# First stage of a four-batch DeltaNet attention and RWKV feed-forward block: a second pair of projection banks, the gates' bias moved to ScalarE, the first norms moved to VectorE, and a new order of steps

## What is computed

```
h  = layernorm(x)
q, k, v = silu(causal_conv4(h @ W{q,k,v}.T))              # 4 taps per channel
beta    = sigmoid(h @ Wb.T)
delta   = delta_rule(l2norm(q), l2norm(k), v, beta)       # a scan over time
local_s, local_m, local_l = causal FIRs of v, 3, 15 and 63 taps per channel
probs = softmax((h @ gate_w + gate_b) / exp(log_temp))    # 5 per head and row
probs = probs * (1 - 5 eps) + eps,  eps = clip(eps_param, 0, 0.2)
o = p0*local_s + p1*local_m + p2*local_l + p3*delta + p4*v
x = x + layernorm(rmsnorm(o) * norm_w @ Wo.T)
r = sigmoid((mu_r*y + (1-mu_r)*y_prev) @ W_r), kk = relu((mu_k*y + (1-mu_k)*y_prev) @ W_k)^2,  y = layernorm(x)
x = x + layernorm(r * (kk @ W_v))
```

## Time and profile before

| | |
|---|---|
| median of 3 runs | 615.87 us (606.55 to 617.87) |
| profiled execution, its own time | 611.72 us |
| its span, first to last instruction | 609.9 us |
| mean granted TensorE clock, share of 2.4 GHz | 0.943 |
| busy: TensorE, VectorE, GpSimd, ScalarE | 84%, 76%, 55%, 45% of the span |

### The profile page before, as it was taken

The page is one execution under the profiler, slowest core; times in us unless marked ns, Lnnn a source line. Parts: engine busy times, 40 slices in busy tenths (PEclk is TensorE's granted clock), DMA queues, the critical chain, the costliest instruction groups (busy, mean ns, idle before and its releaser), DMA issues.

```text
span 609.9 us, 23551 instructions
## 1 busy us (share of the span) xinstructions
PE 512.3 (84%) x9580; PEld 407.8 (67%) x9580; DVE 465.3 (76%) x1182; ACT 276.6 (45%) x688; POOL 336.4 (55%) x408
## 2 busy tenths in 40 slices
PE   2888848999889789798999979899787899888764
PEld 1666636666667567677777767777666777777553
DVE  3788684655589673788899989899768879889863
ACT  5788882111355443435455444454342444433421
POOL 9966202877702440486626378464278776566622
PEclk9999997999999795899999999999888899999978
DMA  9729444699344425341444624165343244333101
GB/s 286 204 71 258 144 139 121 156 225 227 64 73 75 81 63 100 52 72 37 98 88 92 121 52 80 44 120 105 67 72 69 51 104 76 70 80 80 37 17 35
DMA packets 155707, 61.10 MB, mean 100 GB/s; under 512 B 125009, under 2 KB 147409, under 8 KB 155601
## 3 DMA queue, kind: packets, MB, share of 16 engines
q1 hardware_dynamic: 155600, 59.61, 44.5%
HBM read 40.62 MB, written 18.95 MB: 98 GB/s over the span
## 4 chain that ended last, share of the span: by engine, by line
PE 29%; DVE 23%; issue 17%; POOL 13%; SPq 7%; DMA 6%; ACT 3%; POOLq 0%; DVEq 0%; ACTq 0%
PE bank L1864 6%; PE bank L1639 5%; DVE cva L1126 4%; DVE arena L1236 3%; PE bank L1553 3%; POOL arena L659 3%; PE bank L1901 3%; DVE arena L1350 3%; PE bank L1718 2%; DVE arena L1365 2%; DVE arena L1338 2%; POOL seq L650 2%; POOL seq L561 2%; PE bank L1758 2%; POOL seq L648 2%
## 5 line engine op out<-in xcount | busy, mean ns | idle before, releaser
L659 POOL TENSOR_TENSOR arena<-arena,neg_half 128x2 f32<-128x2 f32 (+1 forms) x64 | 61.2, 956 | 148.4 <-DVE arena L1325 88.1
L1236 DVE SCALAR_TENSOR_TENSOR arena<-bank,small,arena 128x256 f32<-128x256 f32 x192 | 89.9, 481 | 15.5 <-ACT arena L898 10.6
L1210 DVE TENSOR_TENSOR seq<-bank,seq 128x384 f32<-128x384 f32 x64 | 35.2, 556 | 30.3 <-PE bank L1639 19.4
L606 POOL TENSOR_TENSOR arena<-seq,powers 128x16 f32<-128x16 f32 x16 | 48.6, 3040 | 17.0 <-DVE seq L1252 17.0
L1639 PE MATMUL bank<-arena 128*64 128x192 f32 x512 | 50.4, 340 | 3.9 <-DVE seq L1210 1.6
L1126 DVE SCALAR_TENSOR_TENSOR cva<-bank,small,cva 128x256 f32<-128x256 f32 x96 | 40.3, 477 | 15.1 <-ACT cva L775 14.8
L577 POOL TENSOR_TENSOR seq<-seq 128x256 f32<-128x256 f32 x32 | 23.3, 729 | 48.2 <-DVE seq L1210 48.2
L1639 PEld LDWEIGHTS bank<-arena 128*64 128x64 f32 x512 | 35.4, 140 | 13.4 <-issue 6.3
L1350 DVE TENSOR_SCALAR arena<-arena 128x256 f32<-128x256 f32 x64 | 31.7, 536 | 16.0 <-POOL arena L659 16.0
L898 ACT ACTIVATE arena<-bank,small 128x256 f32<-128x256 f32 x64 | 29.7, 467 | 26.2 <-PE bank L1718 26.2
L1718 PE MATMUL bank<-arena,w_k 128*128 128x268 f32 x128 | 34.5, 412 | 4.4 <-issue 3.1
(11 more groups left out here) (170 smaller groups left out, 1364.5 us busy)
## 6 DMA issues: line engine op xcount, KB each, us to landing
arena<-v_scratch SPq DMA_DIRECT2D x64, 128.0 KB, 3.3
arena<-fl SPq DMA_DIRECT2D x32, 192.0 KB, 6.4
arena<-fms SPq DMA_DIRECT2D x32, 192.0 KB, 6.8
arena<-xnT_scratch SPq DMA_DIRECT2D x32, 134.0 KB, 3.1
arena<-x SPq DMA_DIRECT2D x32, 128.0 KB, 2.9
gram_scratch<-arena SPq DMA_DIRECT2D x32, 128.0 KB, 2.4
out<-arena SPq DMA_DIRECT2D x32, 128.0 KB
xnT_scratch<-seq SPq DMA_DIRECT2D x2, 1027.0 KB, 6.7
```

The costliest lines, as they stand in the source:

```text
L606: pool.tensor_tensor(rk, ssel[:, slot_of(n)], powers[:, :, :], ALU.pow).then_inc(s["norms"], 1)
L659: pool.tensor_tensor(dst, src, half8 if k == U else neg_half[:, 0:k], ALU.pow).then_inc(s[dst_sem], 1)
L1210: nc.vector.tensor_tensor(fprod[:, q % (2 * FPAIRS), :], bank[fir_bank(q)][:, 0:2 * ROW], fgate[:, q // (TILES // 2), :], ALU.mult).then_i ...
L1236: nc.vector.scalar_tensor_tensor(cv[:, t], ps[:, :, j:j + C], conv_w[:, 1 - t // 2, t % 2, j:j + 1], cv[:, t], ALU.mult, ALU.add).then_inc ...
```

## The change

Only the first stage and the gates are touched, and one stretch between them and the filters.

- The projections use two pairs of banks in turn, (2, 3) for even q and (7, 1) for odd q, and two rows buffers, `cva` and the new `cvx`. `a_proj` now waits for the convolution two blocks back, and `a_tap` for the SiLU of four instructions back. In return the transposes of x have only bank 0.
- `a_norm` of batch 0, blocks 0 and 1, is done by VectorE (`a_first`), right behind `a_row_stats(0, 0)`. GpSimd does the others.
- The gates' bias and temperature are applied in `a_gT_out` on ScalarE, by per-partition scale and bias with the function Identity. The ten VectorE instructions of L1174 fall away; one that multiplies the bias stands in the new `gates_prepared`, behind the first convolution, with the two of L1170 and L1171.
- `gates_mixed`, the last six steps of the softmax, stands inside the sequence (in the same place of VectorE's order).
- The order of the steps on TensorE, ScalarE and VectorE is another one. ScalarE's order per batch differs most at `a_win_out` 4 and 5 and `a_vb` 4 and 5, which now stand before the Exp and the last two SiLUs.
- Ahead of the filters, ScalarE copies `fgate` before it waits for the stores to DRAM, and VectorE does not wait for the stores.

```diff
+        def a_bank(q, oh):
+            return bank[(2, 3, 7, 1)[2 * (q % 2) + oh]]
+        def a_row(q, oh):
+            return (cvx if q % 2 else cva)[:, oh, :]
...
             def rows_of(b, h):
-                if b >= 2:
-                    sp.wait_ge(s["a_normed"], 8 * (b - 2) + 4 * h + 4)
+                if b == 2 and h == 0:
+                    sp.wait_ge(s["a_first"], 4)
+                elif b >= 2:
+                    sp.wait_ge(s["a_normed"], 8 * (b - 2) + 4 * h)
...
             def a_norm(b, q):
+                if b == 0 and q < 2:
+                    return
...
             def a_tap(b, i):
                 act.wait_ge(s["a_proj"], b * 8 + i + 1)
-                act.wait_ge(s["a_vT"], b * 8 + (i - 1 if i >= 2 else 0))
+                if 8 * b + i >= 4:
+                    act.wait_ge(s["a_vT"], b * 8 + i - 3)
...
                 act.wait_ge(s["a_gturn"], b)
-                act.activation(gT, bank[6][:, 0:2 * P], ACT.Copy).then_inc(s["a_gT"], 1)
+                act.wait_ge(s["g_step"], G_READY)
+                act.activation(gT, bank[6][:, 0:2 * P], ACT.Identity, bias=gate_bias, scale=inv_temp).then_inc(s["a_gT"], 1)
...
             # ScalarE, the new order of one turn
             def sequence(b):
                 if 0 <= b - 1 < B:
+                    a_xT_out(b - 1, 1)
+                if 0 <= b - 2 < B:
+                    a_vb(b - 2, 5)
+                    a_vb(b - 2, 4)
+                    gates_exp(b - 2)
+                    a_silu(b - 2, 6)
+                    a_silu(b - 2, 7)
+                if 0 <= b - 1 < B:
+                    a_tap(b - 1, 0)
+                    a_tap(b - 1, 1)
+                    a_xT_out(b - 1, 2)
+                    a_silu(b - 1, 0)
+                    a_xT_out(b - 1, 3)
+                    a_silu(b - 1, 1)
+                    a_tap(b - 1, 2)
+                    a_tap(b - 1, 3)
+                if 0 <= b - 2 < B:
+                    a_vb(b - 2, 6)
+                    a_win_out(b - 2, 6)
+                    a_vb(b - 2, 7)
+                    a_win_out(b - 2, 7)
+                if 0 <= b - 1 < B:
+                    a_silu(b - 1, 2)
+                    a_silu(b - 1, 3)
+                    a_tap(b - 1, 4)
+                    a_gT_out(b - 1)
+                    a_tap(b - 1, 5)
+                    a_win_out(b - 1, 0)
+                    a_vb(b - 1, 0)
+                    a_win_out(b - 1, 1)
+                    a_vb(b - 1, 1)
+                    a_win_out(b - 1, 2)
+                    a_silu(b - 1, 4)
+                    a_tap(b - 1, 6)
+                    a_silu(b - 1, 5)
+                    a_tap(b - 1, 7)
+                    a_vb(b - 1, 2)
+                    a_vb(b - 1, 3)
+                    a_win_out(b - 1, 3)
                 if 0 <= b < B:
+                    a_xT_out(b, 0)
                 if 0 <= b - 1 < B:
                     a_win_out(b - 1, 4)
                     a_win_out(b - 1, 5)
...
             act.wait_ge(s["a_win"], 8 * B)
+            for pr in range(PAIRS):
+                act.wait_ge(s["fgate_mm"], pr + 1)
+                act.activation(fgate[:, pr, :], bank[6 + pr][:, 0:2 * ROW], ACT.Copy).then_inc(s["fgate"], 1)
             act.wait_ge(s["a_gturn"], B)
             for par in ("even", "odd"):
                 act.wait_ge(s[f"xT_{par}_stored"], 16 * 2)
                 act.wait_ge(s[f"vb_{par}_stored"], 64 * 2)
-            for pr in range(PAIRS):
-                act.wait_ge(s["fgate_mm"], pr + 1)
-                act.activation(fgate[:, pr, :], bank[6 + pr][:, 0:2 * ROW], ACT.Copy).then_inc(s["fgate"], 1)
...
+            def a_first(b):
+                if b == 0:
+                    dve.wait_ge(s["a_rs"], 1)
+                    for m in range(4):
+                        nc.vector.tensor_scalar(xna[:, m, :], xa2[0][:, m, :], mv_a[:, m, 0:1], rs_a[:, m:m + 1],
+                                                ALU.subtract, ALU.mult).then_inc(s["a_first"], 1)
...
             # VectorE, the new order: row_stats(0,0), a_first(0), row_stats(0,1), row_stats(1,0), then for each batch
+                    a_conv(b - 26, 0)
+                    gates_ready(b - 26)
+                    a_row_stats(b - 25, 1)
+                    a_conv(b - 26, 1)
+                    a_conv(b - 26, 2)
+                    a_gates(b - 26)
+                    gates_shift(b - 26)
+                    a_conv(b - 26, 3)
+                    gates_sum(b - 26)
+                    a_row_stats(b - 24, 0)
...
-                for g in range(5):
-                    for pr in range(PAIRS):
-                        last = nc.vector.tensor_scalar(gates[:, g, pr, :], gates[:, g, pr, :], gb[:, pr, g:g + 1],
-                                                       inv_temp[:, pr:pr + 1], ALU.add, ALU.mult)
-                then(last)
+                then(nc.vector.tensor_tensor(gate_bias, gate_bias, inv_temp, ALU.mult))
...
             dve.wait_ge(s["a_gate"], B)
-            for par in ("even", "odd"):
-                dve.wait_ge(s[f"xT_{par}_stored"], 16 * 2)
-                dve.wait_ge(s[f"vb_{par}_stored"], 64 * 2)
...
             def a_xT(b, q):
+                if 4 * b + q >= 1:
+                    pe.wait_ge(s["a_xT_out"], b * 4 + q)
...
             def a_proj(b, q):
-                    if b or q:
-                        pe.wait_ge(s["a_conv"], b * 24 + 6 * (q - 1) + 5 + oh)
+                    if 4 * b + q >= 2:
+                        pe.wait_ge(s["a_conv"], b * 24 + 6 * (q - 2) + 5 + oh)
...
             # TensorE, the new order of one batch (its block 0's transposes stand one turn earlier)
+                    a_xT(b - 11, 1)
+                    a_proj(b - 11, 0)
+                    a_xT(b - 11, 2)
+                    a_xT(b - 11, 3)
+                    a_proj(b - 11, 1)
+                if 0 <= b - 12 < B:
+                    a_win(b - 12, 6)
+                    a_win(b - 12, 7)
+                if 0 <= b - 11 < B:
+                    a_gate(b - 11)
+                    a_proj(b - 11, 2)
+                    a_win(b - 11, 0)
+                    a_win(b - 11, 1)
+                    a_gate_turn(b - 11)
+                    a_win(b - 11, 2)
+                    a_proj(b - 11, 3)
+                    a_win(b - 11, 3)
+                    a_win(b - 11, 4)
+                if 0 <= b - 10 < B:
+                    a_xT(b - 10, 0)
+                if 0 <= b - 11 < B:
+                    a_win(b - 11, 5)
```

More of the change, by code:

```diff
@@ L110, in build @@
         norm_w = small[:, 28:29]
-        gb = small[:, 29:39].rearrange("p (r g) -> p r g", r=PAIRS)
-        inv_temp = small[:, 39:41]
-        mix_eps = small[:, 41:43]
+        gate_bias = small[:, 29:30]
+        inv_temp = small[:, 30:31]
+        mix_eps = small[:, 31:33]
         neg_half = sb("neg_half", [P, U])
@@ L562, in a_norm, with sequence @@
                                        ALU.subtract, ALU.mult).then_inc(s["a_normed"], 1)
[L564 to L568, removed]
+            def sequence(b):
+                if 0 <= b - 57 < B:
+                    a_power(b - 57, 0)
+                    a_norm(b - 57, 0)
+                    a_norm(b - 57, 1)
+                    a_power(b - 57, 1)
+                    a_norm(b - 57, 2)
+                    a_norm(b - 57, 3)
+            for b in range(0, 61):
+                sequence(b)
             def fir_sum(h):
@@ L1103, in a_row_stats @@
                 dve.wait_ge(rows_in_sem(b, h), 16 * (b // 2) + 16)
-                if b:
-                    dve.wait_ge(s["a_normed"], 8 * (b - 1) + 4 * h + 4)
+                if b == 1 and h == 0:
+                    dve.wait_ge(s["a_first"], 4)
+                elif b:
+                    dve.wait_ge(s["a_normed"], 8 * (b - 1) + 4 * h)
                 for m in tiles:
@@ L1138, in a_gates, with gates_ready @@
                             nc.vector.tensor_copy(dst[HH[1 - hh], b, :, pr, :, :, par], src[:, NG * h:NG * h + NG]).then_inc(s["a_gate_out"], 1)
+            def gates_ready(b):
+                if b == 0:
+                    gates_prepared()
             def gates_shift(b):
@@ L1166, in _, with gates_prepared @@
             mx4 = gmax[:, :, :].rearrange("p r (w o) -> p o r w", o=1).broadcast_to((P, 5, PAIRS, BLK))
-            def gates_shifted():
-                dve.wait_ge(s["a_gate_out"], 8 * B)
+            def gates_prepared():
+                dve.wait_ge(s["small_in"], 16)
                 dve.wait_ge(s["g_exp"], 1)
@@ L1536, in a_xT @@
             def a_xT(b, q):
-                pe.wait_ge(s["a_normed"], b * 8 + 2 * q + 2)
-                if 4 * b + q >= 2:
-                    pe.wait_ge(s["a_xT_out"], b * 4 + q - 1)
+                if b == 0 and q < 2:
+                    pe.wait_ge(s["a_first"], 2 * q + 2)
+                else:
+                    pe.wait_ge(s["a_normed"], b * 8 + 2 * q - 2)
+                if 4 * b + q >= 1:
+                    pe.wait_ge(s["a_xT_out"], b * 4 + q)
                 for hf in range(HALVES):
```

(7 more changed lines are left out.)

115 lines of the change are left out of this document (41 added, 74 removed).

## The result

The changed kernel takes 608.38 us, median of 20 runs (605.98 to 614.51, and one of 943.74 that nothing on record explains), against 614.92 for the kernel before in as many (606.55 to 620.95). By these medians it is 6.5 us faster. The ratio of the two is 0.9935, 95% interval 0.9910 to 0.9959: 4.0 us faster, within 2.5 to 5.5. This ratio counts of each kernel only the fast runs, those within 1.5% of its fastest, 19 of the changed kernel's and 12 of the other's, which leaves out the upper part of the runs of before and so makes the difference smaller. Forecast were 5.6 us and 608; the two measures stand on either side of the 5.6. The profiled execution has a span of 606.5 us against 609.9.

A forecast was written before the change was run, and what follows sets the result against it. The projection, tap and convolution loop was taken as the limit, three engines close behind. Gains of 1.5 at the start, 2.5 by the last batch, 4.4 at the transposes, 5.6 with 1.18 for stores: 606.1 or 610.3, predicted 608, range 598 to 616.

The forecast's parts named there:

- What bounds it, and the batch: First stage: the new banks open the loop, ScalarE's order (tap 4 behind SiLU 3) closes another; 17.5 us a batch against 17.62.
- E: End of convolution 1 of a batch in the first stage; forecast at 23.0, 40.5 and 58.0 us.
- The start: Batch 0: four norms on VectorE bring the first projection 2.1 us earlier; 1.5 us gained at the end of convolution 1.
- tile 4: Fifth filter tile, from which TensorE is almost full; forecast to start at 97.1 against 102.73, 5.6 us earlier.
- The moved bias: Gates: two pointer operands add 0.17 us to each `a_gT_out`; removing ten VectorE instructions leaves ScalarE late next.
- rival 4: At `a_gT_out`: Identity needs another table than SiLU, so loads cost 10.3 us, 4.7 over the gain, 616.4; chance 0.05.
- Hidden loads: First stage: x for batch 3's first half, behind `v_store(0)`, lands at 48.3, 1.7 us ahead of its statistics.
- The tail: Behind the convolutions: Exp no longer waits for VectorE; last SiLU ends at 87.2 against 91.0, transposes start 4.4 us earlier.
- Had it stayed up: TensorE's clock stays up ahead of the filters: fifth filter tile at 93.9, 8.8 us gained, 603; chance 0.18.
- The stores: Ahead of the filters: removing VectorE's and ScalarE's waits for stores, 6.42 us idle, is worth 1.2 us.
- To the end: Behind the fifth filter tile: later work follows by dependence, so its 5.6 us gain carries to the end unchanged.
- a stretch behind 165 us that is longer or shorter by over a microsecond: Late part of the trace, from 165 us on: such a change in its length would show the forecast wrong.

The follow-up runs named there:

- Exp last: The changed kernel with the gates' Tanh and Exp behind the last two SiLUs on ScalarE: 608.55 us, ratio 0.9841 to the kernel before.
- TensorE kept busy: The changed kernel with 11 matmuls of unused result where TensorE idles ahead of the last transposes: 606.80 us, ratio 0.9802 to the kernel before.
- the delay: The changed kernel with ten useless copies of 1024 columns on ScalarE ahead of its first fgate copy: 620.83 us, ratio 1.0057 to the kernel before.

## Why the prediction was right, and where it was not

**What bounds it, and the batch.** Right in time: E 17.38 and 17.36 us apart, forecast 17.5; without statistics 16.84, forecast 16.9. The reason was half of it. "ScalarE's order does" hold tap 4 back, but with that opened it waited for TensorE's third projection, behind the gates' product. Only both moved gave 16.64 (the projection ahead alone was not run). I had looked for what is late next on ScalarE and not on TensorE.

**The start.** The gain at E of batch 0 is 1.84 us (22.66 against 24.50), forecast 1.5: a norm on VectorE took 0.35 us, not 0.41. But taking the norms back cost 2.6 us there: E was at 25.26, 0.76 behind the kernel before, about what the three steps of `gates_prepared` take ahead of convolution 1 in that run (20.04 to 20.89). So the norms bring 2.6 us and the new order takes part of it back. The rest of the 3.8 at tile 4 is the slow clock of that execution. What the norms would bring in the old order was not run.

**The moved bias.** Forecast as worth nothing, since ScalarE is late next; the ten instructions put back moved tile 4 by 0.17 us. `a_gT_out` took 0.56 against 0.38, the two pointer operands' 0.17 as worked out. This is where rival 4 died: no table load stands at any of them.

**Hidden loads.** A wrong step: x for batch 3 "landing at 48.3, 1.7 us ahead of its statistics". I had set the landing against the statistics' end, E + 9.6, not their start, E + 7.7. It landed at 48.2, VectorE waited 0.55 us, and that lay beneath the tap's lateness: this batch took 17.36 us, the one before it, without such a wait, 17.38. With the faster order the same wait was 2.05.

**The tail.** Last SiLU at 86.90, forecast 87.2; transposes 86.65 against 87.2; tile 0 at 89.64 against 90.1. Tile 4 came 1.3 us before the forecast (95.76 against 97.1). Half a microsecond of it was there at tile 0; the rest is the clock, which was back up in the middle of the gates' matmuls: 1.87 us from their start to tile 2 (92.25 to 94.12) instead of the 2.56 that I took from before, and 1.64 from there to tile 4 instead of 1.82. The clock fell as expected. Had it stayed up, the forecast was 3.2 us; kept up by useless work it was 2.46.

**The stores.** Worth 1.2 us of the 6.42 by forecast, 0.97 measured at tile 4 and 1.26 from tile 0 on.

**To the end.** "I carry what tile 4 gains to the end unchanged": 7.0 us at tile 4, but 3.4 of span in this pair of traces, and 4.0 (2.5 to 5.5) or 6.5 by the runs. Of the 3.6 us between tile 4 and the end of the span 1.0 lies in the filter tables and 2.6 behind the first projection of k. With that a sign that I had named for being wrong has come, "a stretch behind 165 us that is longer or shorter by over a microsecond". What it means is not settled: over the 14 traces that stretch, which no edit touches, lasts from 444.9 to 454.9 us, so that one pair of executions says little. Over the 13 kernels the shift of tile 4 against before (-12.1 to +5.3 us) and the time by the ratio go together with a slope of 0.90, the time being 1.2 us lower on the average than the shift and scattering by 2.7; by the ratio of the medians the slope is 1.02. On the average of these kernels carrying the gain on was a fair rule; whether this one loses any of its 7.0 us, and where, is open.

**The number.** The 5.6 us fell 1.4 short of what tile 4 gained: half a microsecond of that was there at tile 0, and 0.9 is the clock that came back earlier. That 608 was met to 0.4 us is luck in part: it was chosen between 606.1, by the profiled execution, and 610.3, by a median of three runs.

## What to carry to other kernels

When a second buffer opens a loop, write down at once the order of every engine through the same stretch: each step waits for whatever stands ahead of it in line, and here two orders closed the loop again to within 1.5% of its length. Compare a landing with the start of what reads it. And read an idle engine's wait at the engine that sets the end: 6.4 us of it were worth about 1, 2.3 us of removed work nothing, while 5 us of work without use gained 2.5.

## What the runs showed of the hardware

TensorE's granted clock fell to half (1.2 of 2.4 GHz) while the engine was idle, and not after the same idle time: in the kernel before TensorE had been idle since 85.8 us when the clock fell in the window from 90 to 91; in the changed kernel since 81.4 when it fell in the window from 83 to 84 (0.57). It fell also with no idle piece of 3 us: in the run with Exp last TensorE was idle 2.8 us, worked from 85.6, and the clock was 0.53 in the window from 86 to 87, in which it was busy throughout. The Trainium skill (TensorE: Matmul & The Clock Gate, "HAM oscillation — how this bites in real kernels") describes such falls across waits; that one came upon work already resumed is what I had not expected.

It happens at the start too, and not in every execution: with the same code for batch 0, E was at 22.66 and 22.56 in two kernels (the changed one and the one with TensorE kept busy), and at 24.05 and 24.12 in two others (Exp last, and the delay), whose clock was 0.50 from 18 to 20 us. That alone moves an execution by 1.4 us, and a trace of such a kernel should be read against its own E before two are compared.
